# Two attention stages: where the turned shift is copied, and which engine folds the halves of the copied maxima

## What is computed

```python
w = einsum(q, concat(k_strided, k_own_block)) * scale + mask      # layer 0, sparse
o = einsum(softmax(w), concat(v_strided, v_own_block))
scores = where(causal, Q @ K.T / sqrt(Dh), -inf)                  # layer 1, dense, 2 times
y = softmax(scores) @ V
```

## Time and profile before

| | |
|---|---|
| median of 3 runs | 5004.51 us (4998.84 to 5013.22) |
| profiled execution | 5017.06 us, of which the span is 5014.8 |
| PE busy | 4595.3 us (92%) |
| VectorE busy | 3795.4 us (76%) |
| ScalarE busy | 3077.2 us (61%) |
| GpSimd busy | 1515.4 us (30%) |
| mean granted TensorE clock | 0.949 of 2.4 GHz |
| sparse stage, first to last transposed shift | 216 to 776 us |
| dense stage, first to last transposed shift | 1138 to 4220 us |

### The profile page before, as it was taken

The page is one execution under the profiler, slowest core; times in us unless marked ns, Lnnn a source line. Parts: engine busy times, 40 slices in busy tenths (PEclk is TensorE's granted clock), DMA queues, the critical chain, the costliest instruction groups (busy, mean ns, idle before and its releaser), DMA issues. The chain is left out here.

```text
span 5014.8 us, 83754 instructions
## 1 busy us (share of the span) xinstructions
PE 4595.3 (92%) x31872; PEld 2471.4 (49%) x31872; DVE 3795.4 (76%) x8693; ACT 3077.2 (61%) x3565; POOL 1515.4 (30%) x777
## 2 busy tenths in 40 slices
PE   6599997866999999999999999999999998899999
PEld 5355555753443334433334433334433333788888
DVE  8577785766888888888887888888888874655555
ACT  4355654432668876788876778876778876222322
POOL 5200001112455531455531545531445430300000
PEclk9799998886999999999999999999999999899999
DMA  6733323766000301400301400301400000210100
GB/s 189 188 94 82 81 71 107 232 226 116 22 14 12 55 16 26 68 12 11 56 16 26 68 12 6 61 16 25 68 13 6 11 12 11 74 43 22 41 24 9
DMA packets 271626, 280.92 MB, mean 56 GB/s; under 512 B 82488, under 2 KB 202296, under 8 KB 269480
## 3 DMA queue, kind: packets, MB, share of 16 engines
q1 hardware_dynamic: 262460, 228.82, 16.7%
q0 software_dynamic: 6912, 45.22, 5.8%
q10 hardware_dynamic: 1852, 1.53, 0.2%
HBM read 167.92 MB, written 105.97 MB: 55 GB/s over the span
## 5 line engine op out<-in xcount | busy, mean ns | idle before, releaser
L965 ACT ACTIVATE probs_dense<-psum 128x1024 f32<-128x1024 f32 (+3 forms) x2304 | 2078.4, 952 | 618.6 <-PE psum L902 390.3
L1029 DVE TENSOR_REDUCE maxes_dense<-psum 128x1 f32<-128x512 f32 x3152 | 1956.8, 682 | 334.1 <-PE psum L863 331.9
L863 PE MATMUL psum<-keys,queries_dense 62*128 62x512 f32 (+3 forms) x4176 | 1426.2, 450 | 159.6 <-DVE maxes_dense L1022 46.6
L863 PEld LDWEIGHTS psum<-keys,queries_dense 62*128 62x128 f32 x4176 | 636.8, 189 | 1262.6 <-DVE maxes_dense L1029 825.2
L942 PE MATMUL psum<-probs_dense,values 128*32 128x512 f32 (+3 forms) x9216 | 1154.6, 578 | 0.0
L902 PE MATMUL psum<-queries_dense,keys 64*128 64x512 f32 (+3 forms) x4608 | 1059.9, 425 | 34.8 <-ACT probs_dense L965 14.9
L1107 POOL TENSOR_TENSOR max_copies<-max_copies,max_runs 128x1024 f32<-128x1024 f32 x168 | 399.9, 2380 | 1582.6 <-ACT max_copies L982 1582.6
L902 PEld LDWEIGHTS psum<-queries_dense,keys 64*128 64x128 f32 x4608 | 498.9, 188 | 244.4 <-ACT probs_dense L965 101.7
L1022 DVE CUSTOM_DVE_ANT_0 masked_scores_dense<-psum,causal_add 128x128 f32<-128x128 f32 (+3 forms) x1024 | 452.1, 488 | 185.2 <-PE psum L863 178.2
L1109 POOL TENSOR_SCALAR max_copies<-max_copies 128x1024 f32<-128x1024 f32 x168 | 464.9, 2767 | 14.8
L1111 POOL TENSOR_TENSOR max_runs<-max_runs,max_copies 128x1024 f32<-128x1024 f32 x168 | 400.2, 2382 | 14.0
(11 more groups left out here) (305 smaller groups left out, 5921.4 us busy)
## 6 DMA issues: line engine op xcount, KB each, us to landing
v_scratch<-ve_s SPq DMA_DIRECT2D x96, 256.0 KB, 3.5
queries_dense<-parts_scratch SPq DMA_DIRECT2D x384, 64.0 KB
keys<-parts_scratch POOLq DMA_DIRECT2D x42, 512.0 KB, 19.6
parts_scratch<-part_high SPq DMA_DIRECT2D x16, 1024.0 KB, 4.3
parts_scratch<-part_low SPq DMA_DIRECT2D x16, 1024.0 KB, 7.1
values<-v_scratch POOLq DMA_DIRECT2D x8, 2048.0 KB, 44.7
queries_sparse<-parts_scratch SPq DMA_DIRECT2D x192, 64.0 KB
own_keys<-parts_scratch SPq DMA_DIRECT2D x192, 64.0 KB
```

The costliest lines, as they stand in the source:

```text
L863: m = pe.matmul(bank[:, 0:width], q[rows(h, TROWS), h // 2, b * P:(b + 1) * P], k[rows(h, TROWS), h // 2, kc * STRIP:kc * STRIP + width], ...
L965: act.activation(probs[i % 6][:, :, first_col:STRIP], psum[:, at2:at2 + 2, first_col:STRIP], ACT.Exp, scale=SCALE, **extra).then_inc(exp_d ...
L1029: m = dve.tensor_reduce(mx[:, h * BLOCKS + b, kc:kc + 1], bank, AX.X, ALU.max)
```

## The change

It does two things.

**The hand goes through the score banks and ScalarE.** PE transposes `neg_parts` into the next pair of score banks, and ScalarE, not VectorE, copies it to `neg_rows`. So the hand leaves the turns of the side banks and takes a turn in the ring of pairs, on the semaphores `copy_filled` and `copied`, in both stages. `emit_tiles` no longer puts the hand in between tiles: it keeps it in a list `due`, which is emptied before a unit's start and before each chunk's first scores.

**The fold is halved.** After the last merge of a run GpSimd merges columns 256 to 511 of each of the two heads into columns 0 to 255, with three more instructions of 128 x 2 x 256, and only then signals `merged`; VectorE's fold reads 2 x 256 columns.

```diff
@@ emit_tiles @@
                 if before <= of_unit < made and n >= 1:
-                    order.append(("hand", n - 1, None))
+                    due.append(("hand", n - 1, None))
@@ the order, before ("unit", n) and before each chunk's scores @@
+            order += due
+            due = []
@@ pair_users @@
+            elif kind == "hand":
+                copy_at[n, what] = len(copy_at)
+                pair_users.append(("copied", copy_at[n, what] + 1))
@@ attend_pe @@
                     elif kind == "hand":
+                        r = ring_at["copied", copy_at[n, what] + 1]
                         pe.wait_ge(negated, past + n + 1)
-                        pe.transpose(bank[0:MROWS * GROUP * BLOCKS, 0:P], neg_parts[n % 2][:].bitcast(F32).rearrange("p o s h b -> p (o s h b)"),
-                                     ident[:]).then_inc(side_filled, 1)
+                        wait_pair(r)
+                        pe.transpose(psum[0:MROWS * GROUP * BLOCKS, 2 * (r % 2), 0:P],
+                                     neg_parts[n % 2][:].bitcast(F32).rearrange("p o s h b -> p (o s h b)"),
+                                     ident[:]).then_inc(copy_filled, 1)
@@ attend_act @@
+                    elif kind == "hand":
+                        x = copy_at[n, what]
+                        act.wait_ge(copy_filled, past + x + 1)
+                        if n >= 2:
+                            act.wait_ge(queries_in[(n - 2) % 8], handed(n - 2))
+                        act.activation(neg_rows[n % 2][:], psum[0:MROWS * GROUP * BLOCKS, 2 * (ring_at["copied", x + 1] % 2), 0:P],
+                                       ACT.Copy).then_inc(copied, 1)
@@ attend_dve, fold and hand @@
-                                          runs[run % 2][:], AX.X, ALU.max))
+                                          runs[run % 2][:, :, 0:STRIP // 2], AX.X, ALU.max))
...
-                    elif kind == "hand":
-                        e = side_at[kind, n, what]
-                        dve.wait_ge(side_filled, e + 1)
-                        if n >= 2:
-                            dve.wait_ge(queries_in[(n - 2) % 8], handed(n - 2))
-                        dve.tensor_copy(neg_rows[n % 2][:], psum[0:MROWS * GROUP * BLOCKS, 5 + e % 3, 0:P]).then_inc(side_freed, 1)
@@ attend_pool @@
-                        pool.tensor_tensor(run[:], run[:], copy[:], ALU.add).then_inc(merged, 1)
+                        m = pool.tensor_tensor(run[:], run[:], copy[:], ALU.add)
+                        if what[0] == units[n][2] - 1:
+                            pool_chain.then(m)
+                            pool_chain.settle()
+                            near, far = run[:, :, 0:STRIP // 2], run[:, :, STRIP // 2:STRIP]
+                            pool_chain.then(pool.tensor_tensor(far, far, near, ALU.subtract))
+                            pool_chain.settle()
+                            pool_chain.then(pool.tensor_scalar(far, far, 0.0, None, ALU.max))
+                            pool_chain.settle()
+                            m = pool.tensor_tensor(near, near, far, ALU.add)
+                        m.then_inc(merged, 1)
```

More of the change, by code:

```diff
@@ L540, in _build @@
     pv_copied, negated = sem("pv_copied"), sem("negated")
+    copy_filled, copied = sem("copy_filled"), sem("copied")
     def attend(jobs, stage, splits, past):
@@ L625, in emit_tiles @@
                     if n == len(units) - 1:
-                        order.append(("hand", n, None))
+                        due.append(("hand", n, None))
         FOUR = ((2, 3, 3), (4, 6, 6), (10, 12, 13), (15, 15, 16))
@@ L668, in attend @@
         for kind, n, what in order:
-            if kind in ("tile", "hand", "out"):
+            if kind in ("tile", "out"):
                 side_at[kind, n, what] = len(side_at)
@@ L678, in attend @@
                 masks_in = sem("masks_in")
-                copy_filled, copied, merged = sem("copy_filled"), sem("copied"), sem("merged")
+                merged = sem("merged")
             side_filled, side_freed = sem(f"side_filled_{stage}"), sem(f"side_freed_{stage}")
@@ L789, in attend_sp @@
                     elif kind == "hand":
-                        sp.wait_ge(side_freed, side_at[kind, n, what] + 1)
+                        sp.wait_ge(copied, past + copy_at[n, what] + 1)
                         for odd in range(2):
@@ L827, in wait_pair @@
                         name, count = pair_users[r - 2]
-                        pe.wait_ge(copied if name == "copied" else exp_done, count)
+                        if name == "copied":
+                            pe.wait_ge(copied, past + count)
+                        else:
+                            pe.wait_ge(exp_done, count)
                 if sparse:
@@ L970, in attend_act @@
                         at2 = 2 * (ring_at["copied", x + 1] % 2)
-                        act.wait_ge(copy_filled, x + 1)
+                        act.wait_ge(copy_filled, past + x + 1)
                         if kc == 0:
@@ L1042, in attend_dve @@
                         if n >= 2:
-                            dve.wait_ge(side_filled, side_at["hand", n - 2, None] + 1)
+                            dve.wait_ge(copy_filled, past + copy_at[n - 2, None] + 1)
                         high = n3[:, :, 0].rearrange("p o h b -> p h o b")
@@ L1103, in attend_pool @@
                         copy = copies[y % 2]
-                        pool.wait_ge(copied, copy_at[n, what] + 1)
+                        pool.wait_ge(copied, past + copy_at[n, what] + 1)
                         if y >= 1:
@@ L1120, in attend @@
                        (split_done, len(splits[2]))]
-                      + ([] if sparse else [(copied, len(copy_at)), (merged, len(merge_at))]))
+                      + [(copied, past + len(copy_at))] + ([] if sparse else [(merged, len(merge_at))]))
     middle_early = ExitStack()
```

## The result

The changed kernel takes 4955.3 us (median; its undisturbed runs lie from 4952.8 to 4956.2) against 5005.9 for the kernel before on the same chip: a ratio of 0.9895, 95% interval 0.9881 to 0.9909. One execution of the first job took 6843 us with the clock granted at 0.55; it is left out, and the profile of after that is read here is that of a second job (label e1_after_again: 4955.5 us, ratio 0.9897, 0.9883 to 0.9911; profiled execution 4952.7, span 4950.9). Forecast were 4960, and a ratio of 0.9911: 45 us off. Between the medians lie 50.7 us in the first job and 48.7 in the second, and the two ratios make it 52 to 53 of 5005.9.

The account below looks back on a forecast made before the run. PE's queue was taken to set the dense stage's pace, VectorE only in chunks behind folds. Dense 30 + last hands 2 + sparse 9 + clock 4 = 45 us, median 5004.5 to 4960; forecast 4942 to 4978 (chance 0.60), range 4936 to 4999.

Parts of the forecast that it names:

- The fold, 0.61 us a time: Dense stage, VectorE's fold: it reads half as much, so takes 0.61 us less; 0.60 of that gained on PE.
- The hand leaves the side banks, 0.59: Dense stage, the hand's old place: its bank wait and step go away, 0.59 us gained a hand.
- The loss behind the copy, 0.70: Dense chunk with a copy behind the hand: first scores wait for ScalarE's copy, the chunk taking 4.21 us, not 3.51.
- Rival 1: Dense stage: late scores delay exponentials, each of 44 units loses another 0.5 us; about 4990 us; chance 0.17.
- Net a hand: 0.49, masked 0.35: Dense units with fold and copy: net gain 0.49 us at 31 unmasked, 0.35 at 13 masked; dense stage 30 us altogether.
- The first and last hands: First hand comes 26 tiles later at no cost; each stage's last negation wait is partly covered, 2 us in all.
- The sparse stage, 9 us: Sparse stage: 0.2 us from the transpose's free turn and 0.1 from covered DMA waits, 31 x 0.3 = 9 us.
- GpSimd, 4.0 us with 2 to spare: GpSimd's half merge before the fold: three instructions take 4.0 us of 6.0 spare, so 2 us remain.
- Rival 3: Dense folds: a half merge of 7.8 us makes VectorE wait 1.8 at 48 folds; 5046 us; chance 0.04.
- rival 4: Dense stage: more GpSimd work stops VectorE through a shared port, costing over 100 us; 5060 or more; chance 0.02.
- The clock, 4 us with a range of 0 to 20: Dense stage: shorter hold-ups behind folds save a few 3.4 us half-speed stretches, 4 us, from 0 to 20.
- Rival 2: Dense copy chunks: PE's new hold-up at 49 hands brings half-speed stretches, up to 83 us; 5043 us; chance 0.05.

Follow-up runs that it names:

- e3: Kernel before with only the fold halved, the hand staying in VectorE and the side banks: 4975.5 us, 0.9939 of before.
- e10: Changed kernel with VectorE's halved fold done twice: 5001.7 us, 0.9983 of before.
- e6: Changed kernel with the hand in its old place between tiles, still through score banks and ScalarE: 4973.5 us, 0.9929 of before.
- the six other profiles above: Six variants with the changed kernel's sparse stage, instruction for instruction: 0.0 to 26.9 us at half speed there, the stage taking 552.6 to 565.9 us.
- e7: Changed kernel with the middle GpSimd instruction of the half merge done twice: 4952.8 us, 0.9895 of before.
- e8: Changed kernel with the middle GpSimd instruction of the half merge done four times: 5220.3 us, 1.0421 of before.
- e4: Changed kernel with the hand directly behind a chunk's weigh, ahead of the tiles, in both stages: 5118.7 us, 1.0228 of before.
- e2: Changed kernel's hand through score banks and ScalarE, with the kernel before's fold of 1024 columns: 4993.7 us, 0.9975 of before.
- e11: Changed kernel with the hand directly behind the weigh, dense stage only and only where a copy follows: 4949.4 us, 0.9882 of before.

## Why the prediction held, point by point

- **What bounds the chunk behind a fold.** Right: VectorE, before and after (e3, e10), and regular stretches don't move.
- **The fold, 0.61 us a time.** Measured 0.52 to 0.55. 256 columns a head take 0.683 us where 512 took 1.216: some 0.15 of either is fixed, and only the other 1.07 was halved. The step "reads half as much: 0.61 less" took the whole duration for columns, 3 to 4 us too much over 48 folds.
- **The hand leaves the side banks, 0.59.** Measured 0.56 to 0.59 at folds. Without a fold or a copy behind, unit 28's two such chunks gave 0.50 and, at the next, 0.74 (2.91 to 2.17). e6 shows that half of the reason was not in the sum: the place between chunks is needed for it.
- **The loss behind the copy, 0.70.** Measured 0.45 to 0.50. The first scores came at 2.85 as worked out. The step that failed is "two tiles (0.23 apart)" behind them: the two stand at 2483.36 in one record of 0.40, where one tile takes 0.39, and the second scores follow 0.24 later. So two tiles of 62 rows that wait for nothing run beside each other, and the weigh comes 3.97 behind the last one, not 4.21. The trace of before had it already, one chunk ahead of the fold's, scores 0.34 behind the start of a pair of tiles:

```profile
2499.76 0.50 PE L863 MATMUL psum<-keys,queries_dense 62*128 62x512 f32 x2
2500.10 0.40 PE L902 MATMUL psum<-queries_dense,keys 64*128 64x512 f32 x2
```

  The sum put the 0.23 between two tiles on top of that 0.34.
- **Rival 1, the exchange worse than worked out.** Refuted: the first scores behind the copy are late as worked out, and the chunk after it is not (2.13 us before and after), and the loss is 0.45 to 0.50, not 1.2. By its own terms, 22 and the clock's 4 off the 45, it comes to 4986 and not "about 4990".
- **Net a hand: 0.49, masked 0.35.** Measured 0.62 to 0.64 at unit 8 and unit 26, and 0.58 at the masked hand of unit 23 (before 3.78 and 3.58, after 2.67 and 4.11). With 31, 13, 4 and 10 hands of the four kinds the dense sum becomes 31 x 0.64 + 13 x 0.58 + 4 x 1.10 + 10 x 0.57 = 37 us instead of 30; 27 to 34 were found in the middle, and of the 6 us of the first units some 2 (9 us less at half speed have the rest).
- **The first and last hands.** The first hand came 10 us later and cost nothing: SP sends it as soon as the loads ahead of it are issued, at 1154.59 before and at 1151.40 after, and PE goes on 10.2 us behind that in both. At the last hand of each stage PE idles 0.64 and 0.77 us for the negation, where it idled 1.72 and 1.96: 2.3 us, where 2 were forecast.
- **The sparse stage, 9 us.** Wrong as a sum: of the 5 to 6 us that it gave, 2.5 to 4.7 belong to 7 to 9.5 us less at half speed, and 1.0 to the last unit. What is left is a few hundredths a unit. The clock's part is largely chance, as the six other profiles above have it. Two steps failed. "Its turn is free, and 0.2 is saved" read the idle time of a weight load as if the matmul had waited for it. PE's timeline at a hand of the sparse stage after (answers to the earlier trace rows):

```profile
509.95 0.49 PE L864 MATMUL psum<-str_keys,queries_sparse 62*128 62x512 f32 x2
...
510.38 0.09 PEld L890 LDWEIGHTS psum<-ident,neg_parts_sparse 128*32 128x32 f32 x1 [0.24 <-issue]
```

  The transpose no longer waits for anyone and stands 0.43 behind the two tiles as before. That it needs all 128 rows of the array, which the two tiles hold until then, is my reading; no run tested it. It fits that the dense stage's transpose comes 0.33 behind such a pair (2481.51 to 2481.84), where scores of 64 rows come 0.24 behind one. And the DMA waits, 20.0 us at 31 hands, are covered as forecast (16.2 us at 7, the first of them 14.4), but PE's matmuls had been late at only 3 of the 31.
- **GpSimd, 4.0 us with 2 to spare.** Measured 4.2 with 1.7 to spare. It hides, with nothing left for a fourth instruction (e7). Rival 3's point from which it decides, 6.0, and its price are confirmed by e8 (VectorE waits 2.94 us with 4.7 us more on GpSimd and 1.7 to spare), where the clock came on top.
- **The port (rival 4).** Refuted: GpSimd is busy 193 us longer in the dense stage, the tiles' reductions stay at 0.68 to 0.69 us, and e7's 75 us more (48 x 1.57) cost nothing. The Trainium skill (SBUF — State Buffer, "two separate sides") lets the two engines hold each other up at a shared port, on VectorE's side for an instruction in a two-port mode or with two SBUF inputs; the tiles' reductions and the fold have one input, and no run here shows a hold-up for them.
- **The clock, 4 us with a range of 0 to 20.** The mis-sized term. In the middle of the dense stage it was an estimated 13 to 26 us by the traces, and 12 to 20 in the whole program by the clock of all executions. The prediction counted one stretch that begins behind a fold and took a few; 17 to 20 of them were there, most at the same few places in both profiles, and 9 to 12 went.
- **Rival 2, the clock pulled down.** It asked for 27 stretches behind the new hold-up of 0.9 us; 8 in all were found. e8 shows the mechanism to be real: a stop of some 3 us at each fold brings 43. The Trainium skill (TensorE: Matmul & The Clock Gate, "The HAM clock gate") has the full clock depend on the engine's activity, and e8 and e4 agree with it.

Put together: by the two profiles of before, the three stages gave 58 and 65 us. Half-speed time fell by 50 and 70 us in them, at 0.37 to 0.5 worth 18 to 35; the other 30 to 40 us are work no longer waited for, where the forecast had 41. So the work came out at or a little below its sum (the sparse stage too high, the hands in the dense one too low), and the clock well above. The program around the stages took 1 to 3 us more. The median, 4955.3, lies 5 us below the forecast because terms too small (the clock, the hands) outweighed one too large (the sparse stage). That it lies so near is luck in part: the errors have opposite signs.

## What to carry to other kernels

In a kernel whose TensorE is over 90% busy, look for the few places where it stands still for over a microsecond, and note where the clock falls behind them: a wait of 3 us added at each fold cost nearly twice its own length (e8), and shortening such waits gave some clock back as well, though not at any one place that could be foretold. Half-speed time differs between executions of one kernel, so take it from many of them, or from stages whose instructions did not change. When an operation changes the ring of buffers that it takes turns in, its place in the order has to be chosen anew, between two users that come from different chunks; the whole change with the old place gave 0.7% where it gives 1.05% with the new one. Idle time of a weight load is no wait of the matmul behind it, unless the matmul's own record shows one.

## What the runs showed of the hardware

- Hold-ups of PE can cost nearly twice their length: waits of up to 2.94 us before the folds, 133 us in all, cost 265 us (e8). A microsecond at half clock costs 0.34 to 0.37 us in the dense stage (e8, the two profiles of before) and 0.43 to 0.48 in the sparse one (e10, e7); all are estimates from differences of traces.
- Hold-ups of 1.62 to 1.66 us at the ends of units 10, 26 and 42 had a stretch at half speed behind them in 7 of 9 cases (before twice, e2), those of 1.09 to 1.12 in 14 of 21 (after, e3 to e7, e11), and those of 1.8 and of 4.0 us in all six (e10, e8). So the length of the hold-up alone doesn't settle it; what does stays open.
- ScalarE's copy of 32 x 128 from PSUM takes 0.25 to 0.27 us, and GpSimd's merge of 128 x 512 elements 1.27 us (two inputs) and 1.49 (one input and a constant), against 2.38 and 2.77 for 128 x 1024.
